# Delta rule stage: projections written as three fp32r products of high and low parts, with the activations split once per batch

## The reference, cut to what matters

```python
q = short_conv(x @ Wq, conv_q)
k = short_conv(x @ Wk, conv_k)
v = short_conv(x @ Wv, conv_v)
...
u = T @ v
w = T @ kb
...
x_shift = jnp.pad(x, ((0, 0), (dil, 0), (0, 0)))[:, :l, :]
out = out + x_shift * conv_w[i, :, 0] + x * conv_w[i, :, 1]
```

## Time and profile before

| what | value |
|---|---|
| median of 3 runs | 2650.97 us |
| the profiled execution's own time | 2649.22 us |
| its span | 2647.4 us |
| busy, of the span | TensorE 92%, weight loads 76%, VectorE 65%, POOL 51%, ScalarE 46% |
| mean granted TensorE clock | 0.968 of full speed |
| a steady round of the delta rule | 74.2 to 75.2 us |

### The profile page before, as it was taken

The page is one execution under the profiler, slowest core; times in us unless marked ns, Lnnn a source line. Parts: engine busy times, 40 slices in busy tenths (PEclk is TensorE's granted clock), DMA queues, the critical chain, the costliest instruction groups (busy, mean ns, idle before and its releaser), DMA issues. The chain is left out here.

```text
span 2647.4 us, 56555 instructions
## 1 busy us (share of the span) xinstructions
PE 2431.2 (92%) x20838; PEld 2014.3 (76%) x20838; DVE 1711.6 (65%) x4060; ACT 1217.7 (46%) x3095; POOL 1338.6 (51%) x1465
## 2 busy tenths in 40 slices
PE   5999999999999999759999999978899999999998
PEld 3788888888888888537777778856677777777776
DVE  4577677767676767567666766336756747657574
ACT  2666666666666666444544444123333233333332
POOL 3677676767676768166555555215422222322222
PEclk8999999999999999869999999979999999999999
DMA  4000100000000000001122111225021112111211
GB/s 139 7 10 9 44 17 10 10 10 10 10 13 9 7 5 6 13 13 38 46 54 54 41 40 44 64 81 143 23 72 57 49 57 61 61 49 52 64 39 57
DMA packets 156687, 105.03 MB, mean 40 GB/s; under 512 B 85168, under 2 KB 134832, under 8 KB 156416
## 3 DMA queue, kind: packets, MB, share of 16 engines
q1 hardware_dynamic: 131072, 62.83, 8.8%
q10 hardware_dynamic: 25344, 38.60, 4.9%
HBM read 80.51 MB, written 20.88 MB: 38 GB/s over the span
## 5 line engine op out<-in xcount | busy, mean ns | idle before, releaser
L1523 POOL TENSOR_TENSOR m_hid_part<-m_hid,m_hid_part 128x512 fp32r<-128x512 f32 x176 | 239.6, 1361 | 589.6 <-ACT m_hid_part L1434 589.5
L920 POOL TENSOR_TENSOR a_bm<-a_bias,a_mask_add 128x512 f32<-128x512 f32 (+3 forms) x512 | 438.3, 873 | 190.7 <-DVE a_nm L674 186.3
L830 ACT ACTIVATE a_S<-a_S,a_nm 128x512 f32<-128x512 f32 (+3 forms) x512 | 289.3, 565 | 346.7 <-DVE a_nm L674 343.8
L674 DVE CUSTOM_DVE_ANT_0 a_S<-a_S,a_bm,a_nsn 128x512 f32<-128x512 f32 (+3 forms) x512 | 275.6, 545 | 141.5 <-PE a_S L438 137.3
L461 PE MATMUL a_O<-a_v,a_PT 128*128 128x64 f32 x2560 | 342.3, 265 | 0.0
L461 PEld LDWEIGHTS a_O<-a_v,a_PT 128*128 128x128 f32 x2560 | 328.3, 193 | 0.1
L438 PE MATMUL a_S<-a_kT,a_qT 128*128 128x384 f32 (+3 forms) x1024 | 284.2, 359 | 3.5 <-DVE a_nm L674 3.0
L1397 PE MATMUL m_Y<-m_hid_part,m_down_high 128*128 128x512 f32 x704 | 258.6, 408 | 24.9 <-POOL m_hid_part L1523 24.2
L1446 ACT ACTIVATE m_hid<-m_G 128x512 f32<-128x512 f32 x176 | 105.3, 598 | 349.5 <-PE m_G L1380 325.1
L1380 PE MATMUL m_G<-m_in,m_gate_high 128*128 128x512 f32 x704 | 253.0, 400 | 2.5 <-POOL m_up_low L1517 1.6
L1380 PE MATMUL m_U<-m_in,m_up_high 128*128 128x512 f32 x704 | 250.5, 396 | 1.7 <-DVE m_hid L1605 1.7
(11 more groups left out here) (314 smaller groups left out, 5392.8 us busy)
## 6 DMA issues: line engine op xcount, KB each, us to landing
m_spread<-s_w ACTq DMA_DIRECT2D x64, 256.0 KB, 3.2
m_spread<-s_w ACTq DMA_DIRECT2D x128, 128.0 KB, 3.0
a_x<-in_x SPq DMA_DIRECT2D x32, 128.0 KB, 2.1
s_hT<-a_hT SPq DMA_DIRECT2D x32, 128.0 KB, 2.1
d_x<-in_x SPq DMA_DIRECT2D x8, 512.0 KB, 4.7
d_h<-s_hT SPq DMA_DIRECT2D x8, 512.0 KB, 4.0
s_xg<-d_xg SPq DMA_DIRECT2D x8, 512.0 KB, 3.0
d_x<-s_xg SPq DMA_DIRECT2D x8, 512.0 KB, 4.6
```

The costliest lines, as they stand in the source:

```text
L674: dve.tensor_tensor_reduce(S[:, n % S_SLOTS, 0:w], SB[n % 2][:, 0:w], bm[:, n % BM_SLOTS, 0:w], -1.0, nsn[:, tile % 2, h:h + 1], ALU.add, ...
L830: act.activation(S[:, n % S_SLOTS, 0:w], S[:, n % S_SLOTS, 0:w], ACT.Exp, scale=-1.0, bias=nm[:, tile % 2, h:h + 1], accum_out=den[:, tile ...
L920: pool.tensor_tensor(bm[:, n % BM_SLOTS, 0:w], bias[:, h, L - w:L], mask_add[b % 2][:, 0:w], ALU.add).then_inc(s["bm_ready"], 1)
L1523: pool.tensor_tensor(hid_part[1][:, q % H_SLOTS], hid[:, q % G_SLOTS], hid_part[0][:, q % H_SLOTS].bitcast(F32), ALU.subtract).then_inc(hi ...
```

## The change

The weights `wqkv` are split once into a high part (rounded to fp32r by a copy on ScalarE) and a low part (the rest, on VectorE), both during the attention stage. The rows of each batch are split likewise, by a new piece `hs` on ScalarE and on VectorE. A projection is then high weights by high rows, low weights by high rows and high weights by low rows, for two halves of the features: six fp32r matmuls in place of two fp32 ones. Beside that the values `vk` have one buffer in place of two, and the mixer's squares are written back to PSUM, after the copy to `xg`, in place of a buffer `fsq` in SBUF. The SyncE block and the load of `h` are as they were.

```diff
+    w_high = ctx.enter_context(nc.sbuf_tensor("d_wqkv_high", [P, KD, 3 * D], F32R))
+    with nc.sbuf_tensor("d_wqkv", [P, KD, 3 * D], F32) as wqkv:
+        pass
+    w_low = ctx.enter_context(nc.sbuf_tensor("d_wqkv_low", [P, KD, 3 * D], F32R))
...
+                        if t == 4 * TT:
+                            dve.wait_ge(delta["high_ready"], 1)
+                            dve.tensor_tensor(delta["w_low"][:], delta["wqkv"][:], delta["w_high"][:].bitcast(F32),
+                                              ALU.subtract).then_inc(delta["low_ready"], 1)
...
+                        if t == 3 * TT:
+                            act.wait_ge(delta["in"], 16 * len(delta["loads"]))
+                            act.copy(delta["w_high"][:], delta["wqkv"][:]).then_inc(delta["high_ready"], 1)
...
+        TERMS = [(j, s, k) for j, s in ((0, 0), (1, 0), (0, 1)) for k in range(KD)]
...
-            ("qkT", 2, IN), ("uw", 2, F), ("silu", 5, IN),
+            ("hs", 0, NX), ("qkT", 2, IN), ("uw", 2, F), ("silu", 5, IN),
...
-            ("S", 10, R), ("x1", 1, K),
+            ("S", 10, R), ("x1", 1, K), ("hs", 0, NX),
...
-                    "mixer": (frac_copied, TT * b + i + 1), "z": (zm_ready, TT * b + i + 1),
+                    "mixer": (frac_sums, TT * b + i + 1), "z": (zm_ready, TT * b + i + 1),
...
-                        if i == 0 and b > 0:
-                            pe.wait_ge(h_in[b % 2], 16 * ((b + 1) // 2))
+                        if i == 0:
+                            pe.wait_ge(h_high, b + 1)
+                            pe.wait_ge(h_low, b + 1)
                         o = fill(name, i, b)
-                        for k in range(KD):
-                            last = pe.matmul(o[:, :], wqkv[:, k, i * P:(i + 1) * P], h[b % 2][:, k, PAD:],
-                                             start=k == 0, stop=k == KD - 1)
+                        for n, (j, s, k) in enumerate(TERMS):
+                            last = pe.matmul(o[:, :], wqkv[j][:, k, i * P:(i + 1) * P], h_part[s][:, k],
+                                             start=n == 0, stop=n == len(TERMS) - 1)
...
+                    if name == "hs":
+                        if b == 0:
+                            act.wait_ge(delta["h0_in"], 16)
+                        else:
+                            act.wait_ge(h_in[b % 2], 16 * ((b + 1) // 2))
+                            act.wait_ge(proj_psum, 6 * b)
+                        act.copy(h_part[0][:], h[b % 2][:, :, PAD:]).then_inc(h_high, 1)
...
-                        act.activation(fsq[:, i], o[:, 0:D], ACT.Square, accum_out=fss[:, i:i + 1]).then_inc(frac_sums, 1)
                         act.copy(xg[:, i], o[:, 0:D]).then_inc(frac_copied, 1)
+                        act.activation(o[:, 0:D], o[:, 0:D], ACT.Square, accum_out=fss[:, i:i + 1]).then_inc(frac_sums, 1)
...
+                    if name == "hs":
+                        dve.wait_ge(h_high, b + 1)
+                        dve.tensor_tensor(h_part[1][:], h[b % 2][:, :, PAD:], h_part[0][:].bitcast(F32),
+                                          ALU.subtract).then_inc(h_low, 1)
...
-                        if b >= 2:
-                            dve.wait_ge(uw_psum, TT * (b - 1))
+                        if b > 0:
+                            dve.wait_ge(uw_psum, TT * b)
```

More of the change, by code:

```diff
@@ L121, in delta_inputs @@
     t["in"], t["h0_in"], t["loads"] = sem("delta_in"), sem("delta_h0_in"), loads
+    t["high_ready"], t["low_ready"] = sem("delta_high_ready"), sem("delta_low_ready")
     return t
@@ L1673, in delta_phase @@
         sb, bank, sem, sems = space(nc, ctx, "d")
-        wqkv, wsm, smb, conv, frac, cos, sin, rot, mixw, strict, causal, chunk_of, side, eye16, corner, wo, onw, x = (
-            delta[n] for n in ("wqkv", "wsm", "smb", "conv", "frac", "cos", "sin", "rot", "mixw", "strict", "causal",
+        wsm, smb, conv, frac, cos, sin, rot, mixw, strict, causal, chunk_of, side, eye16, corner, wo, onw, x = (
+            delta[n] for n in ("wsm", "smb", "conv", "frac", "cos", "sin", "rot", "mixw", "strict", "causal",
                                "chunk_of", "side", "eye16", "corner", "wo", "onw", "x"))
@@ L1682, in delta_phase @@
         half = sb("half", [P, TT * H2])
+        wqkv = [delta["w_high"], delta["w_low"]]
         h = [delta["h0"], sb("h1", [P, KD, PAD + L])]
+        h_part = [sb(f"h_part{j}", [P, KD, L], mybir.dt.float32r) for j in range(2)]
         xg = sb("xg", [P, TT, D])
@@ L1689, in delta_phase @@
         nb = sb("nb", [P, TT, H2, CH])
-        fsq = sb("fsq", [P, TT, D])
         fss = sb("fss", [P, TT])
@@ L1716, in delta_phase @@
         Z = sb("Z", [P, TT, H2, CH])
-        vk = sb("vk", [P, 2, TT, H2, 2, DH])
+        vk = sb("vk", [P, TT, H2, 2, DH])
         inv = sb("inv", [P, TT, H2, CH])
@@ L1746, in delta_phase @@
         x_in = sem("x_in")
+        h_high = sem("h_high")
+        h_low = sem("h_low")
         proj_psum = sem("proj_psum")
@@ L1966, in _ @@
                 pe.wait_ge(*loaded)
+                pe.wait_ge(delta["low_ready"], 1)
                 pe.wait_ge(delta["h0_in"], 16)
@@ L2057, in _ @@
                                 last = pe.matmul(o[part, j * P:(j + 1) * P], inv[part, i, j],
-                                                 vk[part, b % 2, i, j].rearrange("p a d -> p (a d)"), start=True, stop=True,
+                                                 vk[part, i, j].rearrange("p a d -> p (a d)"), start=True, stop=True,
                                                  tile_position=(c * CH, c * CH))
@@ L2177, in _ @@
                         act.wait_ge(tables_ready, 1)
-                    if name == "proj":
+                    if name == "hs":
[5 more added lines that the diff above has]
+                        act.copy(h_part[0][:], h[b % 2][:, :, PAD:]).then_inc(h_high, 1)
+                    elif name == "proj":
                         o, j, n = RING[place[name, i, b]], i % 3, 6 * b + i
@@ L2344, in _ @@
                             t = 2 * i + tt
-                            ins = dve.tensor_tensor(vk[:, b % 2, t, :, 0],
+                            ins = dve.tensor_tensor(vk[:, t, :, 0],
                                                     o[:, tt * D:(tt + 1) * D].rearrange("p (h d) -> p h d", d=DH),
@@ L2474, in _ @@
                         pool.wait_ge(qk_ready, TT * (b + 1))
-                        if b >= 2:
-                            pool.wait_ge(uw_psum, TT * (b - 1))
+                        if b > 0:
+                            pool.wait_ge(uw_psum, TT * b)
                         for t in range(TT):
-                            pool.tensor_tensor(vk[:, b % 2, t, :, 1], qk[:, 1 + b % 3, t],
+                            pool.tensor_tensor(vk[:, t, :, 1], qk[:, 1 + b % 3, t],
                                                gates[:, b % 3, t, 0:H2].unsqueeze(2).broadcast_to([P, H2, DH]), ALU.mult)\
```

5 lines of the change are left out of this document (3 added, 2 removed).

## The result

The changed kernel takes 2692.9 us, the median of four runs (2680.4 to 2707.5), where the kernel before takes 2649.9 in the same comparison: 1.0162 times as long, 95% interval 1.0103 to 1.022. It is slower, as forecast, but by 43 us and not by 26; the forecast range ended at 2690, and the interval, 2677 to 2708 us, reaches to both sides of that end. The profiled execution of the changed kernel is its slowest (2707.5, span 2705.4), so that what is read from its trace is set against the medians at the end.

A forecast was written before the change was run, and what follows sets the result against it. From 1205 us on, TensorE's own order of work was taken to bound the round. The terms -12.6 + 30 - 2.4 + 4.5 + 1.5 + 5 = +26 on 2649.2 gave 2675 us, range 2660 to 2690.

The forecast's parts named there:

- projections, 36 pieces: Delta-stage projections where TensorE is the round: each of 36 pieces saves about 0.35 us, -12.6 us.
- TensorE's stand, less "issue": TensorE at `attn` 1 and `gram` 0, copies queued behind the load-waiting cast: six loads at 5.0 us, +30, less 2.4.
- start: First projection of the delta stage waits for batch 0's low part: begins 5.7 us later, +4.5 after some is won back.
- weights: Splitting the weights in the attention stage: ScalarE hides nearly all its cast, VectorE's subtraction is waited for; +1.5 us.
- clock: Half clock after TensorE's new stand: a 3.5 us spell costing 1.7 us, in three of six rounds, +5.
- The 2.4 of "issue": TensorE's existing "issue" idle at `gram`, 2.4 us in two rounds, taken to go under in the new stand: -2.4 us.
- The rival from the Trainium skill: Projections: fp32r products stream at 131 ns, a piece takes 0.79 us and saves 0.67 more; 2651 us, chance 0.04.
- The faster one: Load of `h`: ScalarE reaches the cast only after the landing, so wait, stalls and clock's share go; 2640 us, chance 0.06.
- The slower one: Load of `h` lands at its slow end every round, every stall brings half clock: 43 and 12 us, 2695; chance 0.09.
- "Nothing" for `vk` and the squares: Single `vk` buffer and squares in PSUM, in the delta stage: no cost, 0 us.

The follow-up runs named there:

- the filled stand: The control plus unread products on TensorE in the six rounds, 17 ahead of `attn` 1 and seven ahead of `gram` 0: 2679.8 us, 1.0122.
- its control: The changed kernel with VectorE's subtraction of `h` moved behind state update 11, TensorE still standing for the copy of `qkT` 2: 2701.3 us, 1.0173.
- the cast behind the copies: The changed kernel with ScalarE's cast moved behind the copy of `qkT` 3 and VectorE's subtraction behind `low` 0: 2650.5 us, 0.9996 of before.

## Why the prediction was wrong by its size and right in its mechanism

| term | predicted, us | measured, us | from |
|---|---|---|---|
| projections, 36 pieces | -12.6 (-16 to -9) | -10 | 0.28 a piece |
| TensorE's stand, less "issue" | +27.6 | +30.7 | `gram` 0 later behind the load's issue, six rounds; 25.0 of it idle |
| start | +4.5 (2 to 6) | +3.2 | first to second load, 104.6 against 101.4 |
| weights | +1.5 (0 to 3.3) | +3.0 | tile 15 to 29, mean of ten profiles with one subtraction at tile 16 |
| clock | +5 (-6 to 12) | +14 to +21 | the filled stand against its control |
| sum | +26 | +41 to +48 | medians: +43.0 |

The measured terms come from the traces and runs of several kernels; that their sum takes in 43.0 proves none of them alone.

- **The step that failed is the clock.** The prediction put it as "A spell at half clock of 3.5 us costs 1.7; I take it in three of the six rounds". The spell came in all six and lasted 10.2 to 20.5 us, 89 us together in place of 10.5; a microsecond of it cost less than the half that was taken, and together they cost 14 to 21 us. The 3.5 us had been read from one slow projection. In that round TensorE had stood for 1.11 us at `gram` 1, and the projection's long products came as soon as the clock had fallen:

```profile
1423.02 0.59 PE L2035 MATMUL d_R<-d_qkT 64*32 64x32 f32 x45 [1.11 <-issue]
```

What follows the new stand is 7 to 8 us of `attn`, `gram` and `step`, small products through which the clock stayed at half. It came back in the first projection or just behind it in four rounds, behind the second in two. Thirteen long products right behind the stand, 4.9 to 5.5 us of them, ended it sooner.

- **The stand was right**, in its place, its releaser and its length: `gram` 0 starts 1374.98 - 1366.42 = 8.56 us after the load's issue, 3.67 before, so 4.9 late where 5.0 was predicted, and 30.7 in six rounds where 30 were. TensorE stands for 25.0 of these, and `attn` 1, at half clock for a part, takes 1.66 in place of 1.16. The 2.4 of "issue" that were to be swallowed do not show, since the other waits are as long as before. ScalarE's idle time ahead of the cast was 64.9 us in six, 11 each, where some 10 were forecast.
- **The projections were too high.** A boundary between two kinds of product was named as the uncertainty, and 1.57 us in place of 1.47, a saving of 0.28 in the mean, lies towards that end. The rival from the Trainium skill (TensorE: Matmul & The Clock Gate, section Back-to-back issue gap) falls: 1.57 / 6 is 262 ns for 512 columns, twice the 131 ns of its stream.
- **The start** came 5.9 us later behind the beginning of the stage, where 5.7 were predicted; nearly half of it was won back by the second load, by what was not tried. **The weights** cost 3.0 us in the attention stage; the subtraction takes 2.44 on VectorE where 1.8 was estimated from the earlier trace rows.
- **The rivals.** The faster one, the load hidden anyway, did not come; the cast behind the copies is what it would have looked like, at 2650 and not 2640, since the start and the weights eat most of what the products save. The slower one was nearest: it had a spell at every stand, but priced all six at 12 us, and the slow landing it also wanted was not there (median 4.3). That its 2695 lies 2 us from the measured time is luck: 43 for a stand of 31, 12 for a clock of 14 to 21.
- "Nothing" for `vk` and the squares held.

## What to carry to other kernels

When an instruction that waits for a transfer is put into an engine's queue, list what is queued behind it and for whom, and put it behind the last of these: here the place of one cast, and of the subtraction that follows it, is the difference between 1.0162 and 0.9996, and with the first batch's cast moved too the change is worth 0.3% (0.9971). Price a stand of TensorE twice: by its length, and by the half clock after it, whose length here hung on what TensorE did next; take it from a stretch with the same kind of products, not from the quickest return in the trace. Products that fill a stand brought a gain here only when they left no second gap (2679.8 against 2697.8).

## What the runs showed of the hardware that was not expected

- Two gaps of 0.40 and 1.41 us, 1.1 us of products apart, were followed by a fall of the clock (0.91 in the mean of the five rounds); with products in both gaps the mean granted clock was 0.98. In the kernel before one gap of 1.11 us was followed by the slow projection of the earlier trace rows. How short a single gap may be was not tried.
- After the stand the clock stayed at 0.50 for 10.2 to 20.5 us with TensorE busy for most of it (19.68 of 20.50 in the round shown), the first 7 to 8 us on small products. With 13 products of 512 columns (4.9 to 5.5 us) right behind the stand half clock lasted 3.4 to 6.8 us.
- The same subtraction of 128x1536 on VectorE took 2.44 us at tile 16 of the attention stage and 1.75 at its last tile. Why was not tried.
